# Layer 1 of a graph network: three sets of group buffers instead of two

## The reference

```python
s_u = x @ W_u.T + b_u
s_v = x @ W_v.T
e = s_u[src] + s_v[dst]
e = jnp.where(e >= 0, e, 0.2 * e)
m = jax.ops.segment_max(e, dst, num_segments=n_nodes)
e_exp = jnp.exp(e - m[dst])
denom = jax.ops.segment_sum(e_exp, dst, num_segments=n_nodes)
probs = e_exp / denom[dst]
msg = x.reshape(n_nodes, head_dim, num_heads)[src] * probs[:, None, :]
out = jax.ops.segment_sum(msg, dst, num_segments=n_nodes)
x = _layernorm(x + out.reshape(n_nodes, dim), axis=-1)
```

## Time and profile before

| | |
|---|---|
| median of 3 runs | 4833.07 us |
| lowest and highest | 4831.66, 4838.84 us |
| the profiled execution, its span | 4827.7 us |
| layer 1 in it | 3184 to 4606 us |
| TensorE busy | 3239.8 us (67%) |
| GpSimd busy | 3347.0 us (69%) |
| VectorE busy | 1819.0 us (38%) |
| ScalarE busy | 1166.8 us (24%) |
| gathers of layer 1, L1303 | 784, busy 779.9 us |

### The profile page before, as it was taken

One profiled execution on the slowest core, in us unless ns is written; L12 is line 12 of the kernel. 1 busy time (PEld: TensorE's weight loads), 2 busy tenths in 40 slices (PEclk: granted clock), 3 DMA queues, 4 the chain that ended last, 5 costly groups with the idle time before them and its releaser, 6 DMA issues. The chain is left out here.

```text
span 4827.7 us, 62259 instructions
## 1 busy us (share of the span) xinstructions
PE 3239.8 (67%) x14137; PEld 2005.0 (42%) x14138; DVE 1819.0 (38%) x3830; ACT 1166.8 (24%) x3229; POOL 3347.0 (69%) x2982
## 2 busy tenths in 40 slices
PE   3568777777887777778877867845554555555536
PEld 1234444444444444444444435533433333333325
DVE  2543333333333333333333338843333433333315
ACT  0222222222222222222222223312222222222212
POOL 4258888888888888888888868975655555555545
PEclk9878988898889888898898889966666666666667
DMA  7686676666667667666667665645564555555553
GB/s 283 187 279 133 124 136 132 124 130 135 128 127 136 131 124 137 134 124 137 134 124 137 133 142 175 205 126 164 171 191 145 184 164 169 168 167 179 171 171 108
DMA packets 570756, 744.54 MB, mean 154 GB/s; under 512 B 181680, under 2 KB 465396, under 8 KB 566884
## 3 DMA queue, kind: packets, MB, share of 16 engines
q0 software_dynamic: 199136, 338.75, 36.5%
q1 hardware_dynamic: 349440, 364.56, 24.6%
q10 hardware_dynamic: 22148, 40.87, 2.7%
HBM read 442.70 MB, written 301.26 MB: 154 GB/s over the span
## 5 line engine op out<-in xcount | busy, mean ns | idle before, releaser
L813 POOL DMA_INDIRECT S<-l_msum,l_sink x784 | 1282.3, 1636 | 247.3 <-issue 213.9
L1303 POOL DMA_INDIRECT l_feats<-X_rows,l_gsrc x784 | 779.9, 995 | 618.1 <-PE l_psU L1371 335.7
L796 POOL DMA_INDIRECT l_ga<-A_rows,l_gsrc x784 | 793.7, 1012 | 259.3 <-issue 166.4
L886 PE MATMUL l_psU<-l_hid,l_same 128*128 128x257 f32 x1568 | 589.8, 462 | 530.7 <-ACT l_hid L922 498.2
L926 ACT COPY l_msum<-l_psU 128x257 f32<-128x257 f32 x784 | 292.6, 373 | 1894.4 <-POOLq L812 1353.5
L859 PE MATMUL l_psC<-l_table,l_onehot 128*128 x4728 | 727.1, 295 | 0.0
L852 PE MATMUL l_psC<-W1cT,l_attrT 64*128 64x256 f32 x1576 | 620.1, 477 | 10.6 <-DMA l_table<-B_rows 10.6
L1371 PE MATMUL l_psU<-l_feats,l_same 128*128 128x264 f32 x1568 | 491.2, 478 | 151.2 <-DVE l_feats L1452 79.7
L859 PEld LDWEIGHTS l_psC<-l_table,l_onehot 128*128 128x128 bf16 x4728 | 425.8, 104 | 365.9 <-issue 304.5
L886 PEld LDWEIGHTS l_psU<-l_hid,l_same 128*128 128x128 f32 x1568 | 268.0, 214 | 666.5 <-ACT l_hid L922 578.2
L1387 ACT COPY l_part<-l_psU 128x264 f32<-128x264 f32 x784 | 296.0, 378 | 747.1 <-DMA B_rows<-su_zeros 347.2
(11 more groups left out here) (303 smaller groups left out, 3615.0 us busy)
## 6 DMA issues: line engine op xcount, KB each, us to landing
PT<-l_part SPq DMA_DIRECT2D x49, 2176.0 KB
l_srcb<-src_rows SPq DMA_DIRECT2D x99, 512.0 KB
S<-su_zeros ACTq DMA_DIRECT2D x24, 1156.5 KB
l_locb<-loc_rows SPq DMA_DIRECT2D x51, 512.0 KB
l_locb<-loc_rows SPq DMA_DIRECT2D x99, 256.0 KB
nd_sums<-S SPq DMA_DIRECT2D x196, 128.5 KB
l_attr<-in_edge_attr SPq DMA_DIRECT2D x98, 256.0 KB
GH_rows<-l_hidden SPq DMA_DIRECT2D x49, 384.0 KB
```

Of the source, the lines that this page charges most:

```text
L796: pool.indirect_dma_start(ga[:, s, :], None, D["A"], bass.IndirectOffsetOnAxis(ap=gsrc[h][:, j % HALF:j % HALF + 1], axis=0)).then_inc(gat ...
L813: pool.indirect_dma_start(D[f"S{j % NTAB}"], bass.IndirectOffsetOnAxis(ap=sink[j // HALF][:, j % HALF:j % HALF + 1], axis=0), msum[:, j % ...
L886: nc.tensor.matmul(psU[j % 2][:, 0:UW], same[j // HALF][:, j % HALF, :], hid[:, j % RING, :], start=True, stop=True).then_inc(agg_done, 1)
L1303: pool.indirect_dma_start(feats[r][:, t, :], None, D["X1"], bass.IndirectOffsetOnAxis(ap=gsrc[r][:, t:t + 1], axis=0)).then_inc(gathered[r ...
```

## The change

Layer 1 keeps three sets of all group buffers. The loop has three groups in a pass, 16 passes, and the 49th group stands behind it. Before the loop 48 gathers are issued, and the gather released by group g, tile t is that of group g+3. SyncE loads `locb` of group g+3 in the place where it loaded that of g+2, and for the last three groups it only stores. VectorE stages the indices of g+3. At the start GpSimd waits for one staged index at a time. To have enough semaphores, layer 0 clears its own at its end with a block of its own, as setup does already.

```diff
@@ layer 0 @@
-        block = st.enter_context(nc.Block())
+        phase = ExitStack()
+        block = phase.enter_context(nc.Block())
...
+        phase.close()
+        m.clear_sems()
@@ layer 1 @@
-        feats = [m.sb(f"feats{r}", [P, GROUP, XW]) for r in range(2)]
+        SETS = 3
+        feats = [m.sb(f"feats{r}", [P, GROUP, XW]) for r in range(SETS)]
...
         def groups(engine, body, count=NG):
-            with engine.Fori(0, count // 2) as u:
-                for r in range(2):
-                    body(u * 2 + r, r, u, False)
-            if count % 2:
-                body(count - 1, 0, count // 2, True)
+            with engine.Fori(0, count // SETS) as u:
+                for r in range(SETS):
+                    body(u * SETS + r, r, u, False)
+            for r in range(count % SETS):
+                body(count // SETS * SETS + r, r, count // SETS, True)
...
-            def body(g, r, u, last):
-                sp.wait_ge(same_ready, g + 1)
-                dst_rows(r, bass.ds(g * GROUP + 2 * GROUP, GROUP))
+            def store(g, r):
                 sp.wait_ge(part_ready, g * GROUP + GROUP)
                 sp.wait_ge(max_kept, g + 1)
                 sp.dma_start(D["PT"][bass.ds(g * (GROUP * P), GROUP * P), :].rearrange("(t p) w -> p t w", p=P),
                              part[r][:, :, :]).then_inc(stored[r], 16)
-            groups(sp, body)
+            def body(g, r, u, last):
+                sp.wait_ge(same_ready, g + 1)
+                dst_rows(r, bass.ds(g * GROUP + SETS * GROUP, GROUP))
+                store(g, r)
+
+            groups(sp, body, NG - SETS)
+            for g in range(NG - SETS, NG):
+                store(g, g % SETS)
...
-            pool.wait_ge(index_ready, 2)
-            for r in range(2):
+            for r in range(SETS):
+                pool.wait_ge(index_ready, r + 1)
                 for t in range(GROUP):
                     gather(r, t)
...
-                pool.wait_ge(index_ready, g + 3)
+                pool.wait_ge(index_ready, g + SETS + 1)
...
-            groups(pool, body, NG - 2)
+            groups(pool, body, NG - SETS)
...
-                    dst_scores(g + 1, 1 - r, words, 0)
+                    dst_scores(g + 1, (r + 1) % SETS, words, 0)
...
-                stage_index(g + 2, r)
+                if not last:
+                    stage_index(g + SETS, r)
...
-                    find_node(g + 1, 1 - r, u + r)
+                    find_node(g + 1, (r + 1) % SETS, u + (r + 1) // SETS)
```

More of the change, by code:

```diff
@@ L1232, in layer1_phase @@
         m = Mem(nc, st, "l1_")
-        feats = [m.sb(f"feats{r}", [P, GROUP, XW]) for r in range(2)]
-        gsrc = [m.sb(f"gsrc{r}", [P, GROUP], I32) for r in range(2)]
-        locb = [m.sb(f"locb{r}", [P, GROUP, P], BF16) for r in range(2)]
-        onehot = [m.sb(f"onehot{r}", [P, WIN, GROUP, P], BF16) for r in range(2)]
+        SETS = 3
+        feats = [m.sb(f"feats{r}", [P, GROUP, XW]) for r in range(SETS)]
+        gsrc = [m.sb(f"gsrc{r}", [P, GROUP], I32) for r in range(SETS)]
+        locb = [m.sb(f"locb{r}", [P, GROUP, P], BF16) for r in range(SETS)]
+        onehot = [m.sb(f"onehot{r}", [P, WIN, GROUP, P], BF16) for r in range(SETS)]
         svf = m.sb("svf", [P, NB + 1, NH])
@@ L1239, in layer1_phase @@
         table = m.sb("table", [P, NB + 1, NSPLIT * NH], BF16)
-        same = [m.sb(f"same{r}", [P, GROUP, P]) for r in range(2)]
-        part = [m.sb(f"part{r}", [P, GROUP, PW]) for r in range(2)]
+        same = [m.sb(f"same{r}", [P, GROUP, P]) for r in range(SETS)]
+        part = [m.sb(f"part{r}", [P, GROUP, PW]) for r in range(SETS)]
         score = m.sb("score", [P, GROUP, NH])
@@ L1252, in layer1_phase @@
         onehot_ready, sv_done, sv_taken = m.sem("onehot_ready"), m.sem("sv_done"), m.sem("sv_taken")
-        gathered = [m.sem(f"gathered{r}") for r in range(2)]
-        dst_in = [m.sem(f"dst_in{r}") for r in range(2)]
-        stored = [m.sem(f"stored{r}") for r in range(2)]
+        gathered = [m.sem(f"gathered{r}") for r in range(SETS)]
+        dst_in = [m.sem(f"dst_in{r}") for r in range(SETS)]
+        stored = [m.sem(f"stored{r}") for r in range(SETS)]
         index_ready, same_ready = m.sem("index_ready"), m.sem("same_ready")
@@ L1317, in body @@
                     gather(r, t)
-            groups(pool, body, NG - 2)
-            for r in range(2):
-                pool.wait_ge(gathered[r], 16 * GROUP * ((NG + 1 - r) // 2))
+            groups(pool, body, NG - SETS)
+            for r in range(SETS):
+                pool.wait_ge(gathered[r], 16 * GROUP * len(range(r, NG, SETS)))
         @block.tensor
@@ L1408, in compare @@
                                         ALU.is_equal).then_inc(same_ready, 1)
-            stage_index(0, 0)
-            stage_index(1, 1)
+            for r in range(SETS):
+                stage_index(r, r)
             find_node(0, 0, 0)
```

10 lines of the change are left out of this document (5 added, 5 removed).

## The result

| | before | after |
|---|---|---|
| median of 20 runs of each | 4832.52 us | 4845.29 us |
| lowest and highest | 4810.83, 4842.67 | 4828.36, 4857.71 |
| the profiled execution | span 4827.7 | 4830.78, span 4829.1 |

The ratio is 1.0025, with a 95% interval of 1.0015 to 1.0036: slower by 12 us. The forecast was 4831.6, no change. The time lies within its range, but it moved clear of the noise where no change was forecast.

What follows compares the result with a forecast made beforehand. The prediction took layer 1 as a chain of handovers, with TensorE creeping while GpSimd issues gathers. Its terms, 0 + 20 − 16.2 − 5.8 + 0.5 = −1.5 us, took the median 4833.07 to 4831.6, range 4775 to 4872.

Steps and rivals of the forecast that it cites:

- (a): Layer 1's steady state: the third set leaves release times and handover the same, 0 us, with −52 as the other bound.
- (b): Start of layer 1: 48 instead of 32 gathers issued before the first release, +20 us, bounds 0 and +29.
- (c): End of layer 1: gathers stand beside 46 groups instead of 47, −16.2 us, bounds −12 and −18.
- R1: Rival, layer 1: VectorE's waits for gathers to land are on the path, 51.7 us fall, 4780 us; chance 0.14.
- (d): Loop of three: 16 passes, so 8 fewer ScalarE table loads at 0.73 us, −5.8 us, bounds −10.3 and 0.
- R3: Rival, layer 1: GpSimd's backlog covers its pauses, six groups lose 4.9 us each, start costs 9 more, 4870 us; chance 0.15.
- the slow pace: Layer 1 and merge phase: TensorE creeps at 2.9 us a matmul while GpSimd issues gathers back to back.
- (e): Clearing layer 0's semaphores on GpSimd, with a barrier around it: +0.5 us, bounds 0 and +2.
- (f): SyncE's loads of locb and stores of part keep their queue place; GpSimd's initial index wait shrinks under 0.3: all 0.
- R2: Rival, layer 1: with 16 gathers more lead GpSimd never runs dry, about 4550 us; chance 0.08.

## Why the prediction was wrong

The prediction said no change, 4831.6; the kernel is 0.25% slower on the kind of chip that it was made for. The step that failed is (a), which put the third set in the steady state at 0. Start and end, (b) and (c), do cancel: with a lead of three or of two the kernel with three sets takes the same time (1.0024 and 1.0029), and with two sets in the same text it is back at 1.0002. So about 10 us go with the third set outside start and end, and the forecast had -5.8 there. How those us come about is shown in part only. By the forecast's own steps, with the two traces of each kernel on such chips:

- **(a) third set in the steady state, 0.** Wrong, though its reasoning holds for the ordinary groups. The waits for landing fell from 51.7 to 9.7 us and the stage didn't get shorter, so R1 is out. Ordinary distances stayed at 27.9 to 30.5 us and GpSimd's wait for the group's first tile mostly at 5 to 9. But "the release time is the same" was taken for "nothing changes", and that was too much: the pauses of GpSimd changed with the number of sets, from every 112 gathers to every 96 and from 2.63 to 2.25 us.
- **(b) start, +20.** Right in its mechanism, a little too large: 86.2 and 86.7 us from the first gather to the second L1455, against 70.0 and 75.2, +13.8. It showed as 8.5 us before the first L1455 and 5.4 in the first distance, not as a first distance of 49.
- **(c) end, -16.2.** The last three distances sum to 58.5 and 56.8 us, against 73.3 and 73.5: -15.8. Right in size. It is two distances of about 14.5 and not three near 12.7, and single executions scatter: with two sets in the new text it was 70.5.
- **(d) table loads, -5.8.** 16 loads, and a group that begins a pass takes 29.86 us where the others take 29.08 (29.83 and 29.08 in the second trace): 0.8 us each, as the 0.73 of the forecast. But in the trace of two sets in the new text, with its 24 loads, both kinds of group take 29.7 to 29.8, and with three sets and a lead of two they take 29.5. So the term's size isn't settled. If the gain was there in the changed kernel, the next point ate it.
- **The term that is missing: the quick groups.** The 44 distances between start and end sum to 1267.2 and 1257.7 us before, and to 1267.0 and 1269.5 after: +5.8 in place of -5.8. Two groups around a won pause take about 53.5 us, around a lost one 58.5. Six won against four won are 2 x 5 = 10 us of this 11.6. The sum is a mean of few executions that scatter by as much: the two sets in the new text, with all six pauses won, have 1268.0. That is the item of rival R3, which had six such stretches at 5 us each, with a different cause. R3 thought of a backlog that covers the pause. The traces show a pause of 2.25 instead of 2.63 us: the gathers resume 7.22 us after L1455 instead of 7.60. With two sets 24 of 24 pauses are won in four traces, with three sets 12 of 21 in three. That fewer are won with three sets is shown; that the 0.38 us are the reason is argued. In the kernels with two sets the copy of the last tile starts 10.7 to 12.4 us after L1445, in time for the slow pace some 5 us after the pause. With three sets seven of the nine lost pauses have it at 14.4 to 17.3, but two have it at 11.3 and 11.6, and seven of the twelve won ones at 13.0 to 14.4. So the last tile alone doesn't decide.
- **(e) and (f), +0.5 and 0.** Right within what can be told: 1.0002 with two sets in the new text on both kinds of chip.

The sum of the profiled executions is +13.8 - 15.8 + 5.8 = +3.8 us, and layer 1 shows about that: 1424.3 us (mean of two, first gather to last copy) against 1420.0. The timed runs show 10 to 12. The other 6 to 8 us are in no trace. All three traces with three sets are of executions near the lower end of their kernel's runs (4830.8, 4832.6 and 4833.6 us against medians of 4845.3, 4842.5 and 4843.2), and all three have four won pauses. Executions with fewer won pauses would be 5 us longer for each, but none was recorded, so this is argued and not shown.

What would have told: the forecast had read one pause closely and saw that TensorE's quick group hangs on it, but not with how little room. In four traces with two sets the copy of the last tile starts up to 12.4 us after L1445, and the pause's end plus 5 us, about where the slow pace sets in, is 12.6.

The last sentence of the forecast, that the prediction is wrong if the slow pace has another cause than unbroken issuing, is still open in a sharper form. Unbroken issuing goes with the slow pace on the first kind of chip, and on the second GpSimd issues without a break for 1147.6 us and TensorE never slows. So issuing alone is not the cause. By the Trainium skill (SBUF — State Buffer, Who interferes with whom) TensorE's reads have ports of their own, and neither transfers nor GpSimd should slow it. The ten traces of the second kind agree with this rule: no copy comes more than 0.88 us after the one before. Those of the first kind, with copies 1.4 to 4.9 us apart beside the gathers, don't bear it out, though they don't show either that it is the ports. The runs with half rows and with plain transfers, which separate bytes from issuing, didn't meet a chip with the slow pace. That it isn't TensorE's increments on which GpSimd waits was shown by the release by part_ready.

A low clock of TensorE is a rival that the trace of the changed kernel rules out. In the table of windows (columns as in the earlier trace rows) and ScalarE's timeline of one group:

```profile
4110.00:4112.00 2.00, 1.96 (x5) 1.55 (x6) 2.00 (x2) 0.38 (x1) 0.00 (x0) 0.50 0.00 0
...
4118.00:4121.00 3.00, 1.10 (x4) 0.30 (x2) 0.00 (x0) 0.67 (x2) 2.09 (x4) 1.00 0.38 107
...
4128.00:4132.00 4.00, 0.00 (x0) 0.00 (x0) 0.00 (x0) 0.38 (x1) 2.04 (x3) 0.50 0.36 95
...
4112.20 0.38 ACT L1396 COPY l_part<-l_psU 128x264 f32<-128x264 f32 x1 [0.50 <-PE l_psU L1380]
...
4118.56 0.38 ACT L1396 COPY l_part<-l_psU 128x264 f32<-128x264 f32 x1 [1.53 <-issue]
4120.71 0.38 ACT L1396 COPY l_part<-l_psU 128x264 f32<-128x264 f32 x1 [1.78 <-PE l_psU L1380]
```

At a granted clock of 0.50 (1.2 GHz) the first copies of the group come 0.88 us apart. Later, at 1.00 (2.4 GHz), they come 2.15 us apart: the slow pace is there at the full clock. The clock falls to 0.50 afterwards, when the records show TensorE hardly busy (0.00 of 4 us). What the slow pace is stays open.

It is open too why GpSimd pauses every 112 gathers with two sets and every 96 with three. It follows neither the loop's length (four groups a pass: 112) nor the lead (lead of two with three sets: 96).

The forecast named the Trainium skill's rule that all queues share the DMA engines (DMA: Bandwidth & Descriptors, Issuing engines are not separate DMA queues) and put the floor at the DMA time, 782 us, below GpSimd's. With plain transfers layer 1 came to 799 us at a DMA share of 0.91, near that floor, while gathers held it at 1166. The run fits the rule, though no run tells the queues apart. R2's estimate, 4550 us, is close to the time measured where the slow pace is absent (4552), in part by luck: layer 1 takes 1166 us there where R2 had 1143, and the rest of that execution is 17 us shorter than in the kernel before. R2 also put the long gather of the earlier trace rows down to a store. A load of `locb` was issued nearer to it (3786.39, the store at 3784.30), and no run tells which of the two lengthens it.

**A version that beats both.** On a chip with the slow pace the changed kernel with the release by part_ready (0.972 of before) and the one with one wait for four gathers (0.973). On the other kind, three sets with any release tried (0.991 to 0.993). The release by part_ready with three sets was not run there, and with two sets it cost nothing.

## What to carry to other kernels

A deeper buffer pays where someone waits for data on the path. Here that wait was real and fell from 52 to 10 us, but TensorE was late for another reason. As far as the traces explain the price, it came from something that the forecast's sum had left out, a periodic pause of another engine that had helped by chance. When a stage is a race between two engines, count how often the race is won before and after, and how much room there is, and try the moment of the release before the number of buffers: a release 0.4 us later was worth ten times what the third set cost. And measure more than once, at other times and on other chips: here the sign of the change turned between batches (1.0025 and 0.9922).

## What was not expected of the hardware

- One program has two times, 4827 to 4833 us and 4585 to 4589, in different batches; chip number 10 stands beside both. Nearly all of it lies in layer 1, which takes 1407 to 1422 us with two sets on the first kind and 1206 to 1207 on the second. What stands behind it takes 219 to 222 us with either number of sets, and 208 to 211.
- On the first kind TensorE's results come 1.4 to 4.9 us apart from about 5 us after the first of an unbroken run of gathers in layer 1, and later than 7.5 us in the merge phase. The steps between them are multiples of some 0.7 us (1.4, 2.1, 2.8, 3.5, 4.2, 4.9). On the second kind this never happened in 49 groups, in any of ten traces.
- GpSimd pauses at a fixed number of gathers: 112 with two sets of buffers, 96 with three; 2.63 and 2.25 us on the first kind; on the second 2.4 to 7.2 us with two sets, and with three no gap over 0.6 us.
- A gather of 128 rows takes GpSimd 946 ns at 1056 bytes a row and 947 at 528, and a plain transfer of the same bytes 536.
- A loop body of six groups has 55 packets on the queue that fetches instructions, against 22 with three groups, and costs no time that can be told.
